# An already tuned AdaLN kernel of attention and two windowed layers: next group's transposes a slot earlier, VectorE's splits ahead of its chains, other places for the second layer's weights

## The reference

```python
for l in range(2):                      # h: 4 x 1024 x 256
    s = shift_token(h)                  # second half of the features from the token before
    q, k, v = split(s @ wqkv[l])        # 8 heads of 64
    q, k = rotary(l2norm(q) * qs, l2norm(k) * ks)
    o = local_attention(q, k, v)        # windows of 128 tokens: own and previous
    h = h + o @ wo[l]
    s = layernorm(shift_token(h)) * lg + lb
    a, g = split(s @ w1[l] + b1[l])     # 682 hidden features each
    h = h + (a * gelu(g)) @ w2[l] + b2[l]
```

## Time and profile before

| | us |
|---|---|
| median of 3 runs (lowest to highest) | 2208.45 (2204.2 to 2211.89) |
| the profiled execution: its time | 2207.61 |
| the profiled execution: span from first to last instruction | 2205.8 |
| busy PE / VectorE / ScalarE / GpSimd | 1865.4 / 1510.0 / 1186.2 / 996.6 |
| layers, from the first `minima` of group 0 to the end | 722.2 to 2205.8 |
| first `minima` of groups 5, 6, 7, 8, 9 | 1176.9, 1268.1, 1357.3, 1455.8, 1564.3 |

### The profile page before, as it was taken

How to read it: one execution, slowest core, us unless ns; L and a number is a source line. 1 busy time by engine, 2 the same in 40 slices (tenths; PEclk the granted TensorE clock), 3 DMA queues, 4 the chain that set the end, 5 groups by cost and what they waited for, 6 DMA issues and landing times.

```text
span 2205.8 us, 36469 instructions
## 1 busy us (share of the span) xinstructions
PE 1865.4 (85%) x12941; PEld 1403.2 (64%) x12941; DVE 1510.0 (68%) x3723; ACT 1186.2 (54%) x2717; POOL 996.6 (45%) x788
## 2 busy tenths in 40 slices
PE   5569999999954799888899888987888999888986
PEld 3444444444433587776777867766776777777776
DVE  3678878877653685766867758584776857768673
ACT  0545545443433656656566565664656566565562
POOL 0325544647463444444444435543545445454451
PEclk7779999999976999999999999998999999999998
DMA  4000010101024000000000002011000000000000
GB/s 141 24 26 27 1 34 11 41 16 51 15 67 134 11 20 17 19 12 24 20 17 21 10 26 68 17 53 32 25 16 29 27 26 25 18 30 26 26 18 22
DMA packets 83407, 68.58 MB, mean 31 GB/s; under 512 B 10853, under 2 KB 79509, under 8 KB 83225
## 3 DMA queue, kind: packets, MB, share of 16 engines
q1 hardware_dynamic: 83224, 66.25, 9.7%
HBM read 45.22 MB, written 16.81 MB: 28 GB/s over the span
## 4 chain that ended last, share of the span: by engine, by line
PE 35%; DVE 18%; issue 6%; ACT 5%; DMA 2%; SPq 1%; POOL 1%; DVEq 0%; ACTq 0%; POOLq 0%
PE bank_O L1201 4%; PE bank_T L1189 3%; PE bank_A L260 3%; PE bank_A L262 3%; PE bank_P L260 3%; PE bank_A L261 3%; ACT l_sm L1337 3%; PE bank_P L261 2%; PE bank_P L262 2%; DVE l_t L1512 2%; PE bank_A L1178 2%; DVE l_sm L1528 2%; DVE l_u_lo L1594 2%; PE bank_T L1168 2%; PE bank_T L260 1%
## 5 line engine op out<-in xcount | busy, mean ns | idle before, releaser
L1737 POOL TENSOR_TENSOR l_sm<-l_sm,l_rinv 128x512 f32<-128x512 f32 (+1 forms) x256 | 250.1, 998 | 366.1 <-DVE l_rinv L1536 365.8
L1725 POOL TENSOR_TENSOR l_t<-l_qk,l_tab 128x512 f32<-128x512 f32 x128 | 170.1, 1350 | 328.8 <-DVE l_ss L1495 328.8
L1337 ACT ACTIVATE l_sm<-l_sm,l_nb 128x256 f32<-128x256 f32 (+1 forms) x512 | 248.1, 486 | 82.0 <-DVE l_nb L1528 81.8
L260 PE MATMUL bank_A<-l_f_hi,l_w_hi 128*114 128x256 f32 (+1 forms) x768 | 220.1, 287 | 3.7 <-DVE l_f_lo L1573 2.7
L262 PE MATMUL bank_A<-l_f_hi,l_w_lo 128*114 128x256 f32 (+1 forms) x768 | 216.0, 281 | 0.0
L261 PE MATMUL bank_A<-l_f_lo,l_w_hi 128*114 128x256 f32 (+1 forms) x768 | 215.8, 281 | 0.0
L1528 DVE CUSTOM_DVE_ANT_0 l_sm<-bank_A,l_mask 128x256 f32<-128x256 f32 (+1 forms) x512 | 177.1, 401 | 52.0 <-PE bank_A L1178 51.5
L1189 PE MATMUL bank_T<-ident,l_sm 128*128 128x128 f32 x960 | 149.1, 290 | 65.7 <-POOL l_sm L1737 34.4
L618 ACT ACTIVATE pr<-ps_S 128x1024 f32<-128x1024 f32 x128 | 130.7, 1023 | 125.4 <-PE ps_S L512 124.6
L1594 DVE TENSOR_TENSOR l_u_lo<-l_up,l_u_hi 114x256 fp32r<-114x256 f32 (+1 forms) x192 | 197.8, 1036 | 0.1
L861 POOL TENSOR_TENSOR acc<-acc,pr 128x1024 f32<-128x1024 f32 x64 | 155.8, 2435 | 51.0 <-ACT pr L618 46.5
(11 more groups left out here) (268 smaller groups left out, 5127.3 us busy)
## 6 DMA issues: line engine op xcount, KB each, us to landing
l_xs<-x_layers SPq DMA_DIRECT2D x64, 128.0 KB, 2.5
x<-in_x SPq DMA_DIRECT2D x8, 512.0 KB, 3.9
base_rows<-x SPq DMA_DIRECT2D x16, 256.0 KB, 2.1
x_layers<-x SPq DMA_DIRECT2D x16, 256.0 KB, 2.1
l_xs<-x_layers SPq DMA_DIRECT2D x64, 64.0 KB, 2.2
x_layers<-l_yb SPq DMA_DIRECT2D x32, 128.0 KB, 1.8
l_base<-base_rows SPq DMA_DIRECT2D x32, 128.0 KB, 3.1
out<-l_yb SPq DMA_DIRECT2D x32, 128.0 KB, 1.7
```

What stands on the lines that cost most here:

```text
L260: pe.matmul(out, a_hi, b_hi, start=(start and k == 0), stop=False)
L1337: eng.activation(row, row, ACT.Exp, bias=nb[:, R % SS, e:e + 1], scale=-1.0, accum_out=rsum[:, R % SS, e:e + 1]).then_inc(ex_ready, 1)
L1725: eng.tensor_tensor(dst[:, :, :, lo:lo + H2], src[:, :, :, hi:hi + H2], table[:, :, 1, lo:lo + H2].unsqueeze(2).to_broadcast([P, 2, LH, H2 ...
L1737: eng.tensor_tensor(row, row, rinv[:, R % SS, :].unsqueeze(2).to_broadcast([P, 2, P * windows(n)]), ALU.mult).then_inc(pn_ready, 1)
```

## The change

- PE: `qk_transpose` of the group's units 2 and 3 moves from rounds 4 and 6 to rounds 6 and 8 (behind `project` in round 8). `h_transpose` of the next group's second unit moves from slot 1 to slot 0. ScalarE's `qk_out` and `h_out` move with them.
- VectorE: the last `u_split` and the first `y_out` of a group move behind the first `minima` of the next group (rounds 0 and 1); `norms` from round 1 to 3; `rotated` from rounds 3 and 5 to 5 and 7; in slots 0, 2 and 4 `o_split` stands ahead of `inverse`; `h_split` moves from slot 1 to slot 0 ahead of `moments`; `deviation` from slot 1 to 2; `moments`, `norms` and `layer_norm` of slot 8 to slot 7; `rotated` of slots 9 and 10 to slots 8 and 9.
- Weights: `piece_q` one at a time in rounds 5, 6, 7, 8, 10 and 11; `piece_o` in round 4; `piece_1` in rounds 5, 9 and 10; `piece_2` in slots 6, 7 and 8 in place of slot 0, out of two buffers of `pt` and one of `base`; the loads of w2 leave `take_rest` and stand in the queue after the group's third load, where they wait until all `values` of group 8 are done; the second layer's tables in slot 3 in place of round 10.
- GpSimd: `finish` of a group's first two units moves from the group's end to round 2 of the next group.

```diff
-        W_Q = {2: (0, 1), 3: (2, 3), 8: (4, 5)}
-        W_O = {2: (0, 1)}
-        W_1 = {3: (0, 1), 7: (2, 3), 8: (4, 5)}
+        W_Q = {5: (0,), 6: (1,), 7: (2,), 8: (3,), 10: (4,), 11: (5,)}
+        W_O = {4: (0, 1)}
+        W_1 = {5: (0, 1), 9: (2, 3), 10: (4, 5)}
...
+        AT_2 = [pt[:, i, :, :].rearrange("p c n -> p (c n)") for i in range(2)] + pieces[3:4]
...
-                        if r in (4, 6):
-                            qk_transpose(first + 2 + (r - 4) // 2)
                         if r == 8:
                             project(first)
+                        if r in (6, 8):
+                            qk_transpose(first + 2 + (r - 6) // 2)
...
+                        if k == 0 and ahead:
+                            h_transpose(following + 1)
...
-                    if k in ((1, 4, 7) if g >= 0 else (4, 7)) and ahead:
+                    if k in (4, 7) and ahead:
...
+                if n >= QUAD * (GL + 1):
+                    w.wait_ge(w2_ready, 2 + 3)
...
+                        if r == 0 and g >= 1:
+                            u_split(m0 - 1)
+                        if r == 1 and g >= 1:
+                            y_out(2 * g - 2)
+                        if r == 3:
                             norms(first // 2 + 1)
-                        if r in (3, 5):
-                            rotated(first + 2 + (r - 3) // 2)
+                        if r in (5, 7):
+                            rotated(first + 2 + (r - 5) // 2)
...
+                        if k in (0, 2, 4):
+                            o_split(first + 1 + k // 2)
                         if k < 3:
                             inverse(*head(first, r - 2)), inverse(*head(first, r - 1))
-                        if k in (0, 2, 4):
-                            o_split(first + 1 + k // 2)
...
                         if k == 0:
                             residual(first + 1)
+                            if ahead:
+                                h_split(following + 1)
                             moments(first)
                         if k == 1:
-                            if ahead:
-                                h_split(following + 1)
                             moments(first + 1)
+                        if k == 2:
                             deviation(first // 2)
-                        if k == 2:
...
-                        if k == 8:
+                        if k == 7:
                             moments(first + 3)
...
-                    if k == 8 and ahead:
+                    if k == 7 and ahead:
                         norms(following // 2, also=first // 2 + 1 if g >= 0 else None)
...
-                    if k in (9, 10) and ahead:
-                        rotated(following + k - 9)
+                    if k in (8, 9) and ahead:
+                        rotated(following + k - 8)
...
-                        if r == 6 and g >= 1:
-                            finish(first - 2), finish(first - 1)
+                        if r in (2, 6) and g >= 1:
+                            finish(first - 4 + r // 3), finish(first - 3 + r // 3)
...
+            def take_2():
                 w.wait_ge(w1_ready, KC + 6)
+                w.wait_ge(pv_done, PAIRS * QUAD * (GL + 1))
...
                 quarter(2)
+                if g == GL:
+                    take_2()
                 shift(first + 2)
```

34 lines of the change are left out of this document (15 added, 19 removed).

## The result

| | before | after |
|---|---|---|
| median, us (lowest to highest) | 2209.15 (2204.2 to 2211.89) | 2231.85 (2225.45 to 2233.82) |
| ratio, 95% interval | | 1.0098 [1.0082, 1.0115] |
| profiled execution: time, span | 2207.61, 2205.8 | 2225.45, 2223.7 |
| mean granted clock of PE | 0.944 | 0.932 |

A forecast was written before the change was run, and what follows sets the result against it. PE sets the pace, SyncE's queue in group 8. 2207.6 + 11.3 (ordinary groups) + 3.0 (`finish`) - 1.8 - 6 - 2 (groups 7, 8, last) = 2212.1, median 2213 us; own range 2205 to 2221, whole 2178 to 2232.

The forecast's parts named there:

- Rival 2: Slower: w2 pieces hold back `shift` by more than 8 us, twice; 2225 to 2240 us, chance 0.20.
- Rounds 0 to 8: Each group's rounds: `o_split` 0.4 us sooner, `qk_transpose` behind `project` costs 1.1; net 0.8 us lost, bounds 1.0 won, 1.5 lost.
- Slots 0 to 3: Each group's early slots: waits for `h_split` and `o_split` go, smaller ones come; net 1.4 us won.
- Slots 7 to 10: Each group's late slots: `moments` waits 2.2 us for `shift`, `f_split` comes later; net 1.35 us lost.
- Groups 7 and 8: Groups carrying the weight pieces: 1.8 us won in group 7, 6 of 19 us in group 8.
- the ring: Group 8's DMA queue: `shift` stands behind the w2 pieces, so `moments` of slot 5 comes about 8 us late.
- The last group: Final group: wins about 2 us, as its `values` no longer wait for the chain.
- The sum: Whole kernel: 2207.6 + 11.3 + 3.0 - 1.8 - 6 - 2 = 2212.1 us, median 2213.
- wrong the other way: Ordinary groups: the forecast is wrong the other way if PE's clock falls there; no size given.
- Rival 3: Nothing: waits only traded slot by slot, groups 7, 8 and 15 alone count; 2200.6 us, chance 0.06.
- the signs: Next profile: expected waits of `moments`, `p_transpose`, `o_split` and `hidden`; ordinary groups of 90 to 93 us.
- Rival 1: Faster: waits in slots 7 to 10 and rounds 4 to 8 really go; 2160 to 2170 us, half 2187, chance 0.34.

The follow-up runs named there:

- e1: Changed kernel with `moments`, `norms`, `layer_norm` back in slot 8 and `rotated` back in slots 9 and 10: 2195.96 us, 0.9938 of before.
- e5: e1 with each w2 piece of 113 or 114 rows loaded as 112 rows and the rest: 2189.32 us, 0.9906 of before.
- e7: e1 with the edits of e4, e5 and e6 together: 2177.7 us, 0.986 of before.
- e6: e1 with `tables(1)` back in round 10 of group 7 instead of slot 3: 2196.82 us, 0.9951 of before.
- e4: Changed kernel with `shift` issued as two transfers, 112 and 15 rows: 2210.07 us, 1.0011 of before.
- e12: e7 with old rounds and changed end up to group 8, changed rounds and old end later, tables in slot 3: 2170.25 us, 0.9817 of before.

## Why the prediction was right, and where its terms were off

That 2231.85 lies inside the whole range is in part luck. Rival 2 had its condition (`shift` came 10.2 us late, 15.2 less 5.0, where it asked for more than 8), yet group 8 was still 2.6 us shorter than before and adds only 2.7 of the 13.4 us above the forecast. The rest came from slots 7 to 10 with the clock behind them, from the tables, from the last group and from the 3.4 us ahead of group 1.

**Rounds 0 to 8** (0.8 lost in each group, 0.5 more for `finish`). With slots 7 to 10 as before (e1), `minima` of round 10 stands at 26.4 against 26.3 in the odd groups of layer 0 and at 24.7 against 24.3 in the even ones but one (24.9), and at 28.4 against 27.4 in group 11: 0.1 to 0.6 and 1.0 lost, where I had 0.8 and 1.3. The signs hold, the sizes were too large. The 0.8 came from `qk_transpose` behind `project`, priced in full; the positions show no more than 0.4 of it in most groups of layer 0 once the new end is there. Between the layers, where I had put 0.5 for `finish`, groups 5 and 11 differ by 0.9.

**Slots 0 to 3** (1.4 won, bounds 0.8 to 2.9). From `minima` of round 10 to `f_split` of unit 1 it takes 23.9 us before and 22.0 in e1, in both layers: 1.9 won. Right; the two large waits go and less comes back than I took.

**Slots 7 to 10** (1.35 lost). Right in sign, and `moments` waiting 2.2 us and `f_split` 2.1 us late came out within 0.1. Its cost by the runs is 1.6 us in layer 0 and 1.9 in layer 1. Where no lower level follows the wait, though, the part costs 0.6 to 0.7 (groups 5 and 6 against e1's); that level adds the rest in the others; my 1.35 had no clock in it, so its size is partly luck. The step that failed is the place of the first wait: "`up_out` of slot 8, now behind them, ends at 1244.9, and PE wants its bank at 1243.7: about 1.2 us of a new wait". I had named `h_split` as standing behind the chain and then priced only `up_out`. PE waited for `h_split`, 3.4 us. The row that carries the loss was the other one, `rotated` ahead of `f_split`.

**Groups 7 and 8** (won 1.8 and 6, less 0.75 each as for any group). Group 7 lost 3.3. Up to `minima` of round 10 the single pieces win what I gave them: it stands at 28.8 in e1 against 32.8 before, 4.0 sooner, where I had 4.5. (The 7 us that I started from are 7.3; with them it is 4.8, and only so does the sum give 1.8.) From there to `f_split` of unit 1 the ordinary group wins 1.9 and this one loses 3.7 (28.4 against 24.7): the tables in slot 3, which I sized at 3, cost 5.6 by that, and PE's wait there alone is 4.6. Between 101.8 and e1's 99.5 slots 7 to 10 would be 2.3, but e5 took 101.7 with e1's order up to there, so their part of this group stays open. In group 8 `moments` of slot 5 waited 12.7 us where I had "8 us or more"; by the table 2.6 were won of 5.3. Rival 2's place, the ring, was the real one in this group, and e5 gives its price: 8.4 us of group 8.

**The last group** (2 won). It lost 1.4. What I had named came true: PE's wait of `values` for `o_split` falls from 4.2 to 1.6 us, and with slots 7 to 10 undone (e1) the group wins 1.0. What I had left out is the chain of slot 7, ahead of `up_out`: PE waits 7.3 us for it in the changed kernel and 0.3 in e1. `shift`'s landing has nothing in front of it there either; dealt out over more engines it is worth 6.8 us (e7 against e1, 85.2 against 92.0). That term left out the transfer altogether.

**The sum.** The forecast's 4.5 us was too low by 13.4 in the profiled executions: 4.3 in group 7, 2.7 in group 8, 2.6 in groups 9 to 14, 2.7 in the last, 3.4 ahead of group 1, and 2.4 less in groups 1 to 6. I wrote that I would be "wrong the other way if PE's clock falls in ordinary groups": it fell in every window of layer 1 shown above, and in eleven of fourteen groups right behind the 3.4 us wait. The wait doesn't always bring it down: groups 5, 6 and 9 have it and keep the upper level behind it. The 3.4 us ahead of group 1 are not the change's, as far as the runs tell. e1, e5, e6 and e7 do the same up to the first `minima`, but for e7's `shift`, and reach it at 727.0, 726.0, 720.8 and 723.0. The remaining 4.8 us between the two differences (22.7 in the medians, 17.9 in the profiles) have no trace; the three executions after that weren't profiled have a mean granted clock of 0.928 and 0.929, the profiled one 0.932. Rival 3's sum leaves out the last group's 2 us, which it names: 2198.6, not 2200.6.

Of the signs, `moments` of slot 7 came as said (2.19 us), and so did `o_split` under 0.5 (0.43) and group 8's wait. `p_transpose` of round 2 waited 0.94 in group 5 and 2.57 in group 11 (1 to 1.6 said); the wait in slot 9 was for `h_split`, not for `up_out` or `f_split`; ordinary groups took 89.0 to 94.1 us (90 to 93 said).

Rival 1 decided "where `moments` of slot 7 waits under 1 us". e4 took that wait away, and the gain still didn't come, since GpSimd held the chain. That condition was too weak. The upper end of its time, 2160 to 2170, is what e12 reaches (2170.25), with the moved chain and `rotated` taken out.
